# A graph-network kernel on one core: closing loops, clears and block sums moved between engines, front-stage loads spread over more buffers

## The reference, cut to what matters

```python
h = maximum(layernorm(x), 0)
x = x + conv(h, node_vec1, src, dst, edge_attr_4, edge_attr_8)   # h0, h1 = h @ W_lin1; gather by src; times weights of
                                                                 # silu(edge_attr_8 @ fc_w0) @ fc_w1 and harmonics;
                                                                 # segment_sum by dst; @ W_lin2; plus a skip h @ W_sc
h = maximum(layernorm(x), 0)
for l in range(2):                                               # two attention layers
    z = (h @ W[l]).reshape(n, 4, 64)
    e = leaky_relu(el[src] + er[dst], 0.2)                       # el, er: z times al, ar, summed
    alpha = segment_softmax(e, dst)
    h = elu(segment_sum(z[src] * alpha, dst) + h + b[l])
x = x + h
```

## Time and profile before

| | us |
|---|---|
| median of 3 runs | 3375.71 (3372.01 to 3376.48) |
| profiled execution | 3369.64 |
| its span, from first to last instruction | 3367.9 |

### The profile page before, as it was taken

How to read it: one execution, slowest core, us unless ns; L and a number is a source line. 1 busy time by engine, 2 the same in 40 slices (tenths; PEclk the granted TensorE clock), 3 DMA queues, 4 the chain that set the end, 5 groups by cost and what they waited for, 6 DMA issues and landing times. The chain is left out here.

```text
span 3367.9 us, 77082 instructions
## 1 busy us (share of the span) xinstructions
PE 2813.5 (84%) x20204; PEld 1753.1 (52%) x20205; DVE 2281.9 (68%) x6599; ACT 1638.6 (49%) x5990; POOL 2460.4 (73%) x2634
## 2 busy tenths in 40 slices
PE   7788888888888868898988889885888888888887
PEld 5455555555555545555555555543555454554544
DVE  7688888888888746666666666664666665665666
ACT  6333333333333345555555555543555555555554
POOL 7677777777777657777777777746777777777774
PEclk9889988998889855555555555555555555555555
DMA  7555555555555445555555555545555555555553
GB/s 249 172 161 157 162 158 157 157 158 155 159 161 159 146 134 160 154 153 157 154 156 157 154 156 154 155 115 144 153 153 157 153 156 154 153 156 158 157 157 111
DMA packets 286668, 524.58 MB, mean 156 GB/s; under 512 B 88657, under 2 KB 139925, under 8 KB 286495
## 3 DMA queue, kind: packets, MB, share of 16 engines
q0 software_dynamic: 119808, 334.13, 36.2%
q1 hardware_dynamic: 166815, 189.94, 17.9%
HBM read 436.48 MB, written 87.36 MB: 156 GB/s over the span
## 5 line engine op out<-in xcount | busy, mean ns | idle before, releaser
L1712 POOL DMA_INDIRECT nodes<-z_rows,scratch x1664 | 1585.8, 953 | 584.9 <-issue 486.5
L1131 POOL DMA_INDIRECT scratch<-h_rows,scratch x832 | 800.3, 962 | 264.6 <-issue 250.6
L1672 ACT ACTIVATE nodes<-nodes 128x64 f32<-128x64 f32 x3296 | 808.6, 335 | 0.1
L1789 PE MATMUL ge_part<-nodes,scratch 128*32 128x260 f32 x3328 | 448.9, 632 | 49.6 <-ACT nodes L1672 49.1
L1279 DVE TENSOR_TENSOR nodes<-ce_w,scratch 128x768 f32<-128x768 f32 x416 | 377.1, 948 | 0.0
L1174 PE MATMUL ce_part<-nodes,scratch 128*32 128x128 f32 (+1 forms) x6656 | 313.0, 336 | 55.5 <-DVE nodes L1279 55.4
L1155 PE MATMUL ce_w<-fc_sb,scratch 64*128 64x256 f32 x1664 | 260.9, 436 | 97.3 <-ACT scratch L1043 97.3
L1969 DVE TENSOR_TENSOR nodes<-nodes,ge_part 128x512 f32<-128x512 f32 x416 | 267.3, 684 | 96.8 <-ACT nodes L1655 96.8
L1682 ACT COPY scratch<-ge_part 128x260 f32<-128x260 f32 x208 | 78.1, 375 | 454.5 <-PE ge_part L1789 452.1
L1174 PEld LDWEIGHTS ce_part<-nodes,scratch 128*32 128x32 f32 x6656 | 200.5, 121 | 160.7 <-DVE nodes L1279 77.7
L1155 PEld LDWEIGHTS ce_w<-fc_sb,scratch 64*128 64x128 f32 x1664 | 160.5, 207 | 223.7 <-issue 169.6
(11 more groups left out here) (278 smaller groups left out, 4962.6 us busy)
## 6 DMA issues: line engine op xcount, KB each, us to landing
scratch<-places SPq DMA_DIRECT2D x208, 256.0 KB
nodes<-z_rows,scratch POOLq DMA_INDIRECT x1664
nodes<-hT SPq DMA_DIRECT2D x56, 256.0 KB
scratch<-h_rows,scratch POOLq DMA_INDIRECT x832
places<-nodes SPq DMA_DIRECT2D x52, 256.0 KB
places<-lin_sb SPq DMA_DIRECT2D x52, 256.0 KB
z_rows<-scratch SPq DMA_DIRECT2D x28, 264.0 KB
z_rows<-nodes SPq DMA_DIRECT2D x28, 264.0 KB
```

The costliest lines, as they stand in the source:

```text
L1131: nc.gpsimd.indirect_dma_start(xg[u][:, i * D:(i + 1) * D], None, m.h_rows, bass.IndirectOffsetOnAxis(ap=idx[r][:, k:k + 1], axis=0)).then ...
L1672: ins = nc.scalar.activation(head_rows(r, k, h), head_rows(r, k, h), ACT.Copy, scale=zg[r][:, at:at + 1])
L1712: nc.gpsimd.indirect_dma_start(zg[r][:, k * ZW:(k + 1) * ZW], None, m.z_rows[layer], bass.IndirectOffsetOnAxis(ap=idx[r][:, k:k + 1], axis ...
L1789: ins = nc.tensor.matmul(ps_part[j * TW:(j + 1) * TW, 0:D + HEADS], one_hot(hot[r], k), zg[r][:, k * ZW:k * ZW + D + HEADS], start=(q == 0 ...
```

## The change

Front stage: x has 18 places (8 old ones and 10 in the part of `nodes` that is cleared last). A load is issued ten blocks ahead, before the store of the block. 25 blocks are run; for the 26th zeros are stored from a cleared part of `nodes`. The eight `lin1` loads are issued by ScalarE, ahead of its first block. Of `src`, `dst` and `sh` only the part of the first 8 groups is loaded; the rest is loaded in the convolution stage, where ScalarE waits for it once. The flags are stored once, and the convolution stage's SyncE copies them four times from memory to memory. 13 of the 26 pieces of `nodes` are cleared by ScalarE (as a copy of a zero column) after its blocks 1 to 5, 13 by GpSimd after its blocks 6 to 24. The attention columns' loads are spread over more blocks.

Convolution: `take_sums` and `clear_sums` of the quads are on ScalarE, behind its copy of the step's sums; VectorE waits for the clearing in the next step. In all edge stages the first index copy has a fixed place and stands first on ScalarE.

Attention: `exponential` has two passes, and `elu` takes the -1. In the closing loop `elu` comes before `clear_sums`, the second load waits for nothing, and the last quad's row store is issued by ScalarE.

```diff
@@ front_stage, SyncE
-                r = n % X_SLOTS
-                if n >= X_SLOTS:
-                    sp.wait_ge(st_skip[r], 16 * (n // X_SLOTS))
-                sp.dma_start(b.x[r], pairs_of(io["x"], n)).then_inc(x_in[r], 16)
+                before = n - X_SLOTS - MORE
+                if before >= 0:
+                    sp.wait_ge(st_skip[before % X_SEMS], 16 * (before // X_SEMS + 1))
+                sp.dma_start(b.x[n], pairs_of(io["x"], n)).then_inc(x_in[n % X_SEMS], 16)
...
-            for n in range(NPB):
+            for n in range(BLOCKS):
+                if FIRST_LOADS <= n + AHEAD < BLOCKS:
+                    load(n + AHEAD)
                 between(n)
                 store(n)
-                if X_SLOTS <= n + 6 < NPB:
-                    load(n + 6)
@@ front_stage, ScalarE
+            def zero(n):
+                ins = nc.scalar.copy(m.nodes[:, n * 4 * PB:(n + 1) * 4 * PB], blank.broadcast_to([P, 4 * PB]))
+                if n == 0:
+                    ins.then_inc(s_blank, 1)
...
+            first_layer()
...
+                for k in CLEARED_BY_ACT.get(n, ()):
+                    zero(k)
@@ conv_stage, SyncE
             load(0)
+            for edges, name, w in edge_arrays(m):
+                sp.dma_start(edges[:, EARLY * w:], m.io[name][:, EARLY * w:]).then_inc(edges_in, 16)
             sp.wait_ge(hid_ps, 1)
             load(1)
+            for_head = m.tile_flags.rearrange("(g h e) j -> h g (e j)", h=HEADS, e=G + 1)
+            for h in range(HEADS):
+                sp.dma_start(for_head[h], m.group_flags).then_inc(st_flags, 16)
@@ conv_stage, ScalarE
+            def take_sums(n, k, windows, b=node):
+
+                act.wait_ge(s_pT, k + 1)
+                act.wait_ge(added, windows).then_inc(act_go, 1)
+                nc.scalar.copy(chunks(b.y, 4), node_cols[:, :, bass.ds(n * PB, PB)]).then_inc(y_in, 1)
+
+            def clear_sums(n, k):
+
+                act.wait_ge(y_in, k + 1).then_inc(act_go, 1)
+                nc.scalar.copy(node_cols[:, 0:3, bass.ds(n * PB, PB)],
+                               node.zero.rearrange("p (c o) -> p c o", c=1).broadcast_to([P, 3, PB])).then_inc(cleared, 1)
...
+                if r == 0:
+                    n = load_block(act, m, quad)
+                    take_sums(n, quad, quad * 4 + 2)
+                    clear_sums(n, quad)
...
+            act.wait_ge(edges_in, 48)
             all_steps(act, last_quad, step)
@@ conv_stage, VectorE
+                if r == 1:
+                    dve.wait_ge(cleared, quad + 1).then_inc(dve_go, 1)
                 add_window(v - 1)
...
-                if r == 0:
-                    take_sums(slot.n, quad, quad * 4 + 2)
-                    clear_sums(slot.n, quad)
@@ gat_stage, SyncE
-            def load_second(n, k):
-                sp.wait_ge(s_den, k)
+            def load_second(n):
...
-                if r == 3:
+                if r == 3 and ahead >= 4:
                     store_rows(slot.n, quad)
@@ gat_stage, ScalarE
-                nc.scalar.activation(b.h, b.h, ACT.Exp, scale=-1.0).then_inc(s_ex, 1)
-                act.wait_ge(s_ex, k + 1)
-                nc.scalar.activation(b.ps[:, :], b.h, ACT.Copy, bias=-1.0).then_inc(s_em, 1)
+                nc.scalar.activation(b.ps[:, :], b.h, ACT.Exp, scale=-1.0).then_inc(s_em, 1)
...
+                if r == 3 and last:
+                    n = load_block(act, m, quad)
+                    act.wait_ge(s_rows, quad * ROWS + 2 * ROWS)
+                    nc.scalar.dma_start(*rows_out(n, node)).then_inc(st_rows, 16)
@@ gat_stage, VectorE
-                V.scalar_tensor_tensor(b.hT, b.x, 0.0, b.ps[:, :], ALU.max, ALU.add).then_inc(s_hT, 1)
+                V.scalar_tensor_tensor(b.hT, b.ps[:, :], -1.0, b.x, ALU.add, ALU.max).then_inc(s_hT, 1)
...
+                elu(k)
+                elu(k + 1, second)
                 if layer == 0:
                     clear_sums(n)
                     clear_sums(n + 1)
-                elu(k)
-                elu(k + 1, second)
```

More of the change, by code:

```diff
@@ L164 @@
 X_SLOTS = 8
+MORE = 10
+FREE = 3 * NC // (4 * PB)
+X_SEMS = 13
+AHEAD = 10
+FIRST_LOADS = AHEAD
+CLEARED_BY_ACT = {1: range(0, 1), 2: range(1, 5), 3: range(5, 7), 4: range(7, 11), 5: range(11, 13)}
+CLEARED_BY_POOL = {6: 13, 7: 14, 8: 15, 9: 16, 10: 17, 12: 18, 13: NPB - 1}
+BLOCKS = NPB - 1
 ROW_SLOTS = 3
@@ L203, in front_stage @@
         b = Mem()
-        b.x = [part(P, PAIRS) for _ in range(X_SLOTS)]
+        early = [part(P, PAIRS) for _ in range(X_SLOTS)]
+        more = [m.nodes[:, at:at + PAIRS] for at in range(3 * NC, 3 * NC + MORE * PAIRS, PAIRS)]
+        b.x = early + more + [early[n % X_SLOTS] for n in range(BLOCKS - X_SLOTS - MORE)]
         b.h = [part(P, PAIRS) for _ in range(2)]
@@ L461, in _ @@
             counters()
-            for n in range(NPB + 0):
-                if n < NPB:
-                    hidden(n)
+            for n in range(BLOCKS):
+                hidden(n)
                 if n == 1:
@@ L468, in _ @@
                     heads()
-                elif n == 12:
+                elif n == 19:
                     attention()
-                if n < NPB:
-                    zero(n)
+                if n in CLEARED_BY_POOL:
+                    zero(CLEARED_BY_POOL[n])
+                elif n >= 14 and n % 2 == 0:
+                    k = FREE + (n - 14) // 2
+                    last = min(X_SLOTS + MORE, X_SLOTS + 1 + 2 * (k - FREE))
+                    for block in range(X_SLOTS if k == FREE else last - 2, last):
+                        pool.wait_ge(st_skip[block % X_SEMS], 16 * (block // X_SEMS + 1))
+                    zero(k)
         @block.tensor
@@ L544, in _ @@
             pair_scales()
-            for n in range(1, NPB + 2):
-                if n - 1 < NPB:
+            for n in range(1, BLOCKS + 2):
+                if n - 1 < BLOCKS:
                     transposes(n - 1)
@@ L724, in _ @@
             done(V.memset(ones_row, 1.0))
-            for n in range(NPB + 3):
-                if n < NPB:
+            for n in range(BLOCKS + 3):
+                if n < BLOCKS:
                     statistics(n)
@@ L753, in _, with first_layer @@
         def _(act):
+            def first_layer():
+                act.wait_ge(s_zero, 1)
+                for c in range(2):
+                    for half in range(2):
+                        rows = slice(half * MUL, half * MUL + MUL)
+                        at = half * MUL
+                        scalar_part = c == 0 and half == 0
+                        nc.scalar.dma_start(m.lin1[rows, c, at:at + MUL],
+                                     io["W_lin1_0" if scalar_part else "W_lin1_1"]).then_inc(s_lin1, 16)
+                        nc.scalar.dma_start(m.lin1[rows, c, 2 * MUL + at:2 * MUL + at + MUL],
+                                     io["W_sc0" if scalar_part else "W_sc1"]).then_inc(s_lin1, 16)
             def deviation(n):
@@ L1524, in head_rows, with rows_out @@
             return zg[r][:, at:at + HF]
+        def rows_out(n, b):
+            if layer == 0:
+                return rows_of(m.z_rows[1], n), tile(b.rows, ZW)
+            return rows_of(m.io["out"], n), tile(b.rows)
         @block.sync
```

156 lines of the change are left out of this document (83 added, 73 removed).

## The result

| | before | after |
|---|---|---|
| median us | 3374.27 (3372.01 to 3376.48, 4 runs) | 3348.10 (3347.93 to 3348.62, 4 runs) |
| profiled execution us | 3369.64 | 3348.07 |
| its span us | 3367.9 | 3346.3 |

The ratio is 0.9926, with an interval of 0.9914 to 0.9938: 26.2 us faster. The forecast was 3351.2 us, in a range of 3343 to 3363.

What follows compares the result with a forecast made beforehand. GpSimd's gathers were taken to bound all three edge loops, so only time outside them could be won. Terms of -13.6 (front stage), -4, 0, -1.2, -4.3 and -1.4 summed to -24.5 us: 3375.71 to 3351.2, range 3343 to 3363.

Steps and rivals of the forecast that it cites:

- Waits for x: Front stage: with loads issued earlier, VectorE's 19.6 us of waits for x fall to near 4, -13.9 us.
- what is late next: Front stage, after the loads of x: DMA engines at 2.4 us a block against VectorE's 2.23, 4 us put back.
- First weights on ScalarE: Front stage: eight weight loads issued by ScalarE delay its first step by 3.0 us, +2.3 us in the sum.
- Convolution: Convolution loop: moving VectorE's 37 us of copies to ScalarE wins only the stretching of gathers, -4 us.
- Edge arrays and flags: Convolution's start: edge array loads and flag copies beside the first gathers are covered, 0 us, up to 5 if not.
- First index copies: Start of each of three edge stages: ScalarE's first copy comes earlier, 0.4 us each, -1.2 us.
- Closing loops: Ends of both attention layers: earlier loads and a shorter ELU, with ELU before the clears in the first; -4.3 and -1.4 us.
- Rival D: Closing loops: loads come no earlier because SyncE is held elsewhere; -1.5 us together, 3355 us; within the forecast's chance of 0.63.
- A: Front stage stays bound by transfers: 3359 us, or 3362 with ScalarE's early clears uncovered too; chance 0.17.
- B: Whole kernel: everything comes, no front-stage waits come back and all gather stretching goes, 3343.7 us; chance 0.10.
- C: Convolution loses GpSimd's pace through take-out and clearing on ScalarE, beyond 6 us a quad of delay; 3403 us; chance 0.04.
- E: Convolution: VectorE's copies hold GpSimd for their whole length, so all 37 us go, 3318 us; chance 0.01.

Runs made afterwards that it cites:

- the short lead: The changed kernel with loads of x issued six blocks ahead instead of ten, the 18 places kept: 3355.05 us.
- the extra copies: The changed kernel with one more 256 KB memory-to-memory DMA of x behind each front-stage block's stores, 25 in all: 3359.14 us.
- a delay of 9.4 us: The changed kernel with eight more ScalarE copies of the taken-out sums ahead of the real one in every quad of the convolution: 3633.27 us.

## Why the prediction was right, point by point

*Waits for x.* The mechanism was right: they went from 19.6 us to 1.9, below the forecast 4, and came back with the short lead. The size was not, as far as the traces tell. VectorE's last skip ended at 93.26 in the profiled execution and at 93.2 in the mean of seven, against 101.97 before: some 8.8 us, not 13.6. (Of the kernel before there is one trace, and it is its fastest execution; if its front stage happened to be a short one, more was won. What follows on the waits does not hang on that.) The step that failed is "what is late next". I looked for it in the DMA engines alone and put 4 us back. There were two more things. The diff moves the attention columns from turns 13 to 16 of TensorE to turns 20 to 23, with their last load only at SyncE's turn 15; I read it as a spreading of loads and priced it at nothing. And TensorE needs 2.2 us a block itself, as much as VectorE, so a wait removed on one engine is partly filled by one for another (the short lead: 11 us of waits for 4 to 6 us of time). The second is borne out by that run. What the late columns cost was not seen in time: the two kernels that move loads and columns up took the wait for the bias away and ended within the spread.

*First weights on ScalarE.* Sized at +2.3, and VectorE's third statistics were 2.8 us later (8.77 for 5.97). But it was given back: undone, it brought 0.6 us at the last skip against the mean, which is nothing within the spread. Right in place, too large in the sum. The sum gave the move nothing for bandwidth, and the traces show none gained. In the first 10 us the changed kernel moves 242 GB/s and the kernel with `lin1` on SyncE 121, since SyncE goes straight on to the loads of x, but in the next 10 it is 127 against 251, so that both have moved the same by 20 us.

*One block fewer, the clears, and the flags and edge arrays taken out of the stage* were not tested apart. ScalarE's 13 clears took 1.05 us each on average; the estimate was 1.0.

*Convolution.* Forecast -4, measured -3.3, and -4.0 to -4.6 from the kernel that undoes it. The 37 us of VectorE's time were worth only the stretching of gathers.

*Edge arrays and flags.* Forecast 0: no gather of the convolution waits over 0.32 us.

*First index copies.* Forecast -1.2, measured -2.0.

*Closing loops.* Layer 0 forecast -4.3, measured -4.30 on the chain; layer 1 -1.4, measured -1.28. Rival D is out.

*Rivals.* A holds for a part of the front stage, as the extra copies show. B's 3344 did not come. C did not happen. Its price was wrong: of a delay of 9.4 us it let 6 be absorbed, and some 2 were, with 3.5 more for the clock. E is excluded: its hold of GpSimd for the copies' whole length is shown by no run; with the copies on VectorE again the gathers took 4.0 to 4.6 us more, not 37.

*The starting point.* The sum on the two traces is 21.6 us, 2.9 less than forecast, and yet the medians differ by 24.4 and 26.2, as much as was forecast. The profiled execution of before, 3369.64, was faster than all 24 others that were timed with the experiments and the result (3370.12 to 3378.13). The prediction took its terms from that trace and set their sum against the median, 6.1 us higher. From the trace it would have been 3345.1, 3.0 too low; from the median it is 3351.2, 3.1 too high. Both lie in the range, so that is not what made it right; but that the sum agrees with the difference of the medians is in part luck, since nothing in the traces shows the other 3 to 5 us.

## What to carry to other kernels

When one engine's gathers set the pace, work taken off another engine is worth only what it stretched the gathers (here 3.3 us of gathers for 37 us of VectorE's copies); look for time at the stage's ends, where a chain of a few instructions can be followed from row to row and its parts add up. A wait that is removed from an engine that others keep pace with is worth less than its length; here it was about half. And every instruction that a diff moves has to be priced at its new place, also where it looks like tidying: what waits for it, and whether its input is there.

## What the runs showed that I had not expected

Equal instructions in the front stage ended up to 4.8 us apart (90.7 to 95.5), and the gaps between stages 2 to 3 us. TensorE's mean granted clock in the convolution fell from 0.91 to 0.80 when it was held for 9.3 us once a quad. In the quad shown it was 0.51 in the 15 us behind the stall and 1.00 in the 4.6 us after them. By the account above, which is worked out from means, this is why a delay of 9.4 us cost 10.6, more than itself. The same happened on a small scale in the front stage, where a stall of 1.4 us was followed by products at 0.50 (79.5 to 81.0).
